# An attention block on one core: only the layer norm's result is turned, and the RMS factor moves to the values and to the floor of the norms

## The reference, cut to what matters

```
xn  = (x - mean) / sqrt(var + 1e-5)                      # layer norm, no weights
xh  = xn * rsqrt(mean(xn^2) + 2^-23) * norm_w            # RMS norm inside the attention
q, k, v = xh @ Wq, xh @ Wk, xh @ Wv                      # [256, 1024] each
q = q / max(|q|, 1e-12) * (q_gamma + 1) * 8              # per head
k = k / max(|k|, 1e-12) * (k_gamma + 1) * 8
p = softmax(tanh(q k^T / 50) * 50 / 8)
out = x + (p v) @ Wo + ffn(xn)
```

## Time and profile before

| | |
|---|---|
| instructions | 34237 |
| POOL busiest line | L1014, 256 times 1895 ns, 485.1 us |
| ACT busiest lines | L612 and L619, 256 times each, 265.4 and 272.8 us |
| longest waits, whole span | PEld L552 on issue 53.0 us, DVE L796 on PE 47.3 us, ACT L612 on PE 37.1 us |
| DMA | 85.44 MB moved, 310492 packets, 42.8% of the engines' time on the main queue |

### The profile page before, as it was taken

How to read it: one execution, slowest core, us unless ns; L and a number is a source line. 1 busy time by engine, 2 the same in 40 slices (tenths; PEclk the granted TensorE clock), 3 DMA queues, 4 the chain that set the end, 5 groups by cost and what they waited for, 6 DMA issues and landing times.

```text
span 1067.6 us, 34237 instructions
## 1 busy us (share of the span) xinstructions
PE 1033.9 (97%) x12889; PEld 844.5 (79%) x12889; DVE 938.0 (88%) x2217; ACT 976.3 (91%) x1417; POOL 981.2 (92%) x912
## 2 busy tenths in 40 slices
PE   6689999999999999999999999999999999999997
PEld 4468888888888888888888888888888888888877
DVE  5888999989999989999988999988999998999972
ACT  3689999999999999999999999999999999999996
POOL 6699999999999999999999999999999999999883
PEclk9899999999999999999999999999999999999999
DMA  3244434444453345544445444345444444444451
GB/s 117 46 86 73 90 81 73 76 87 82 85 81 80 72 84 86 82 82 76 83 76 87 84 80 81 72 86 90 79 82 82 77 78 90 77 86 73 72 99 31
DMA packets 310492, 85.44 MB, mean 80 GB/s; under 512 B 282021, under 2 KB 309817, under 8 KB 310329
## 3 DMA queue, kind: packets, MB, share of 16 engines
q1 hardware_dynamic: 310328, 83.25, 42.8%
HBM read 11.09 MB, written 4.19 MB: 14 GB/s over the span
## 4 chain that ended last, share of the span: by engine, by line
PE 43%; POOL 27%; issue 9%; SPq 6%; DVE 6%; ACT 4%; DMA 4%; POOLq 0%; ACTq 0%
POOL probs_lo L1014 11%; PE ps_scores L526 9%; PE ps_y L574 5%; PE ps_aux L501 4%; POOL sq_k L995 4%; POOL halves L1006 4%; PE ps_o L552 4%; PE ps_aux L512 4%; PE ps_aux L446 4%; DMA heads_T<-halves 3%; SPq L411 3%; PE ps_y L572 3%; PE ps_aux L448 3%; PE ps_aux L447 3%; SPq L399 2%
## 5 line engine op out<-in xcount | busy, mean ns | idle before, releaser
L1014 POOL TENSOR_TENSOR probs_lo<-probs 128x1024 f16<-128x1024 f32 x256 | 485.1, 1895 | 20.0 <-ACT probs L619 18.7
L612 ACT ACTIVATE clamped<-ps_scores 128x1024 f32<-128x1024 f32 x256 | 265.4, 1037 | 44.3 <-PE ps_scores L526 37.1
L619 ACT ACTIVATE probs<-clamped 128x1024 f32<-128x1024 f32 x256 | 272.8, 1066 | 3.0 <-PE ps_o L554 0.4
L552 PEld LDWEIGHTS ps_o<-v_hi,probs 128*128 128x128 bf16 x2048 | 183.9, 98 | 57.3 <-issue 53.0
L526 PE MATMUL ps_scores<-heads_T 64*128 64x256 f16 x3072 | 212.5, 271 | 5.3 <-ACT clamped L612 3.1
L552 PE MATMUL ps_o<-v_hi,probs 128*128 128x65 bf16 x2048 | 214.8, 195 | 2.8 <-POOL probs_lo L1014 1.6
L553 PE MATMUL ps_o<-v_lo,probs 128*128 128x64 bf16 x2048 | 212.4, 193 | 0.0
L554 PE MATMUL ps_o<-v_hi,probs_lo 128*128 128x65 bf16 x2048 | 211.8, 194 | 0.0
L446 PE MATMUL ps_aux<-w_hi,xhT_hi 128*128 128x512 f32 x384 | 176.1, 459 | 13.5 <-DVE qk L824 9.1
L553 PEld LDWEIGHTS ps_o<-v_lo,probs 128*128 128x128 bf16 x2048 | 187.8, 99 | 0.0
L554 PEld LDWEIGHTS ps_o<-v_hi,probs_lo 128*128 128x128 f16 x2048 | 187.7, 97 | 0.0
(11 more groups left out here) (85 smaller groups left out, 2001.8 us busy)
## 6 DMA issues: line engine op xcount, KB each, us to landing
heads_T<-halves SPq DMA_TRANSPOSE x512, 2.5
x_in<-in_L_attn_tokens_dram SPq DMA_DIRECT2D x32, 128.0 KB, 2.4
x_res<-in_L_attn_tokens_dram SPq DMA_DIRECT2D x32, 128.0 KB, 2.3
out_dram<-y_sb SPq DMA_DIRECT2D x32, 128.0 KB, 2.0
sel_raw<-xn SPq DMA_DIRECT2D x192, 4.0 KB
qk<-in_L_attn_Wkv_dram SPq DMA_DIRECT2D x2, 512.0 KB, 5.6
qk<-in_L_attn_Wq_dram SPq DMA_DIRECT2D x1, 512.0 KB, 3.6
qk<-in_L_ffn_W_dram SPq DMA_DIRECT2D x2, 256.0 KB
```

Source lines behind the costliest of these rows:

```text
L552: pe.matmul(full, hi[:, col], v_hi[:, par, u, h], start=(u == 0), stop=False)
L612: nc.scalar.activation(clamped[:].rearrange("p j n -> p (j n)"), ps_scores[:].rearrange("p j n -> p (j n)"), ACT.Tanh).then_inc(clamp_done, 1)
L619: nc.scalar.activation(probs[:, pair % RING].rearrange("p j n -> p (j n)"), clamped[:].rearrange("p j n -> p (j n)"), ACT.Exp, bias=LIFT, ...
L1014: g.tensor_tensor(probs_lo[:, buf].rearrange("p j n -> p (j n)"), probs[:, buf].rearrange("p j n -> p (j n)"), probs[:, buf].rearrange("p ...
```

## The change

xh is no longer made. Only xn is turned (two transposes instead of four), and ACT copies the same PSUM tile twice, into the fp32r tile for the projections and into the fp32 tile for the feed-forward block. The RMS factor, rstd[1], now is (1/(var+eps) * (var (1 + 2^-23) + 1e-5 2^-23))^-1/2, a number near one, and is multiplied in where v leaves PSUM: on ACT as the scale of an activation, on DVE as the scalar of a scalar_tensor_tensor. For q and k the floor of the squared norms is multiplied by the inverse of its square instead (`norm_floor`), one number for each token.

The two additions that POOL did before its power move to DVE's `norm_var`, in slot 4 behind the statistics and ahead of the read of q0, with a reciprocal and a product of two tiles; all four work on two elements for each partition, in SBUF. POOL keeps the power and adds one instruction for the floor. rstd and norm_floor are kept for four batches. The first instruction of `seed` becomes two, one for each token tile.

```
@@ norm tiles
-        rstd = sb("rstd", [P, 2, TT])
+        ms_eps = sb("ms_eps", [P, TT])
+        inv_eps = sb("inv_eps", [P, TT])
+        rstd = sb("rstd", [P, 4, 2, TT])
+        norm_floor = sb("norm_floor", [P, 4, TT])
-        xh = sb("xh", [P, TT, P])
@@ PE, aux "xT"
                     for t in range(TT):
-                        pe.transpose(bank[:, t * P:(t + 1) * P], xh[:, t], ident[:])
-                    for t in range(TT):
-                        ins = pe.transpose(bank[:, seq + t * P:seq + (t + 1) * P], xn[:, par, t], ident[:])
+                        ins = pe.transpose(bank[:, t * P:(t + 1) * P], xn[:, par, t], ident[:])
@@ ACT, aux
+                if kind == "v" and k == 0:
+                    act.wait_ge(rstd_made, b + 1)
-                    nc.scalar.copy(xnT[:, b % 3], bank[:, seq:2 * seq]).then_inc(xnT_copied, 1)
+                    nc.scalar.copy(xnT[:, b % 3], bank[:, 0:seq]).then_inc(xnT_copied, 1)
-                    nc.scalar.copy(v_hi[:, par, t, 8 * c:8 * c + 8, 0:DH],
-                                   bank.rearrange("p (h d) -> p h d", d=DH)).then_inc(v_hi_made, 1)
+                    nc.scalar.activation(v_hi[:, par, t, 8 * c:8 * c + 8, 0:DH],
+                                         bank.rearrange("p (h d) -> p h d", d=DH), ACT.Copy,
+                                         scale=rstd[:, b % 4, 1, t:t + 1]).then_inc(v_hi_made, 1)
@@ DVE, norm_var, behind its bn_aggr
+                dve.wait_ge(meanvar_made, 2 * b + 2)
+                wait(dve, floor_made, b)
+                v.tensor_scalar(var_eps[:, 0], mean_var[:, :, 1], LN_EPS, None, ALU.add).then_inc(vareps_made, 1)
+                v.tensor_scalar(ms_eps[:], mean_var[:, :, 1], 1.0 + RMS_EPS, RMS_EPS * LN_EPS,
+                                ALU.mult, ALU.add).then_inc(vareps_made, 1)
+                dve.wait_ge(vareps_made, 2 * b + 2)
+                v.reciprocal(inv_eps[:], var_eps[:, 0]).then_inc(inveps_made, 1)
+                dve.wait_ge(inveps_made, b + 1)
+                v.tensor_tensor(var_eps[:, 1], ms_eps[:], inv_eps[:], ALU.mult).then_inc(ratio_made, 1)
@@ DVE, seed
-                    v.tensor_scalar(minus_half_norm2, norm2[:], NORM2_MIN, -0.5, ALU.max, ALU.mult)\
-                        .then_inc(seed_made, 1)
+                    dve.wait_ge(floor_made, b + 1)
+                    half_of = TT * HEADS
+                    for t in range(TT):
+                        part = slice(t * half_of, (t + 1) * half_of)
+                        v.tensor_scalar(minus_half_norm2[:, part], norm2[:, part], norm_floor[:, b % 4, t:t + 1], -0.5,
+                                        ALU.max, ALU.mult).then_inc(seed_made, 1)
@@ DVE, aux "v"
-                    v.tensor_tensor(v_lo[:, par, t, 8 * c:8 * c + 8], bank.rearrange("p (h d) -> p h d", d=DH),
-                                    v_hi[:, par, t, 8 * c:8 * c + 8, 0:DH], ALU.subtract).then_inc(v_split, 1)
+                    v.scalar_tensor_tensor(v_lo[:, par, t, 8 * c:8 * c + 8], bank.rearrange("p (h d) -> p h d", d=DH),
+                                           rstd[:, b % 4, 1, t:t + 1], v_hi[:, par, t, 8 * c:8 * c + 8, 0:DH],
+                                           ALU.mult, ALU.subtract).then_inc(v_split, 1)
@@ POOL, norm_rstd
-                pool.wait_ge(meanvar_made, 2 * b + 2)
-                wait(pool, rstd_made, b)
-                g.tensor_scalar(var_eps[:, 0], ...).then_inc(vareps_made, 1)
-                g.tensor_scalar(var_eps[:, 1], ...).then_inc(vareps_made, 1)
-                pool.wait_ge(vareps_made, 2 * b + 2)
+                pool.wait_ge(ratio_made, b + 1)
                 wait(pool, xn_made, b)
+                wait(pool, v_split, 4 * (b - 3))
                 g.tensor_tensor(rstd[:, b % 4]..., var_eps..., minus_half[:], ALU.pow).then_inc(rstd_made, 1)
+                wait(pool, seed_made, 3 * (b - 3))
+                g.tensor_scalar(norm_floor[:, b % 4], var_eps[:, 1], NORM2_MIN, None, ALU.mult).then_inc(floor_made, 1)
@@ POOL, norm_apply
-                g.tensor_tensor(xn[:, par], x_mid[:], rstd[:, 0]..., ALU.mult)
-                g.tensor_tensor(xh[:], x_mid[:], rstd[:, 1]..., ALU.mult).then_inc(xn_made, 1)
+                g.tensor_tensor(xn[:, par], x_mid[:], rstd[:, b % 4, 0]..., ALU.mult).then_inc(xn_made, 1)
```

More of the change, by code:

```diff
@@ L274, in block_kernel @@
         seed_made = sem("seed_made")
+        ratio_made = sem("ratio_made")
+        inveps_made = sem("inveps_made")
+        floor_made = sem("floor_made")
         newton_step = sem("newton_step")
@@ L738, in seed @@
                     wait(dve, newton_step, 9 * b)
-                    v.tensor_scalar(minus_half_norm2, norm2[:], NORM2_MIN, -0.5, ALU.max, ALU.mult)\
-                        .then_inc(seed_made, 1)
+                    dve.wait_ge(floor_made, b + 1)
[4 more added lines that the diff above has]
+                                        ALU.max, ALU.mult).then_inc(seed_made, 1)
                 else:
-                    dve.wait_ge(seed_made, 2 * b + 1)
+                    dve.wait_ge(seed_made, 3 * b + 2)
                     v.tensor_scalar(newton_r[:].bitcast(I32), minus_half_norm2.bitcast(I32), -0.5, RSQRT_SEED,
@@ L749, in newton @@
                 if k == 0:
-                    dve.wait_ge(seed_made, 2 * b + 2)
+                    dve.wait_ge(seed_made, 3 * b + 3)
                 wait(dve, newton_step, 9 * b + k)
@@ L826, in aux @@
                 elif kind == "v":
+                    if k == 0:
+                        dve.wait_ge(rstd_made, b + 1)
                     dve.wait_ge(v_hi_made, 4 * b + k + 1)
                     t, c = k // 2, k % 2
-                    v.tensor_tensor(v_lo[:, par, t, 8 * c:8 * c + 8], bank.rearrange("p (h d) -> p h d", d=DH),
-                                    v_hi[:, par, t, 8 * c:8 * c + 8, 0:DH], ALU.subtract).then_inc(v_split, 1)
+                    v.scalar_tensor_tensor(v_lo[:, par, t, 8 * c:8 * c + 8], bank.rearrange("p (h d) -> p h d", d=DH),
+                                           rstd[:, b % 4, 1, t:t + 1], v_hi[:, par, t, 8 * c:8 * c + 8, 0:DH],
+                                           ALU.mult, ALU.subtract).then_inc(v_split, 1)
                 elif kind == "low":
@@ L922, in norm_rstd @@
                 b, _, _ = st.batch(ahead)
-                pool.wait_ge(meanvar_made, 2 * b + 2)
-                wait(pool, rstd_made, b)
-                g.tensor_scalar(var_eps[:, 0], mean_var[:, :, 1], LN_EPS, None, ALU.add).then_inc(vareps_made, 1)
-                g.tensor_scalar(var_eps[:, 1], mean_var[:, :, 1], 1.0 + RMS_EPS, RMS_EPS * LN_EPS,
-                                ALU.mult, ALU.add).then_inc(vareps_made, 1)
-                pool.wait_ge(vareps_made, 2 * b + 2)
+                pool.wait_ge(ratio_made, b + 1)
                 wait(pool, xn_made, b)
-                g.tensor_tensor(rstd[:].rearrange("p a b -> p (a b)"), var_eps[:].rearrange("p a b -> p (a b)"),
+                wait(pool, v_split, 4 * (b - 3))
+                g.tensor_tensor(rstd[:, b % 4].rearrange("p a b -> p (a b)"), var_eps[:].rearrange("p a b -> p (a b)"),
                                 minus_half[:], ALU.pow).then_inc(rstd_made, 1)
+                wait(pool, seed_made, 3 * (b - 3))
+                g.tensor_scalar(norm_floor[:, b % 4], var_eps[:, 1], NORM2_MIN, None, ALU.mult).then_inc(floor_made, 1)
             def norm_apply(st, ahead):
@@ L940, in norm_apply @@
                 pool.wait_ge(mid_made, b + 1)
-                g.tensor_tensor(xn[:, par], x_mid[:], rstd[:, 0].unsqueeze(2).to_broadcast([P, TT, P]), ALU.mult)
-                g.tensor_tensor(xh[:], x_mid[:], rstd[:, 1].unsqueeze(2).to_broadcast([P, TT, P]), ALU.mult)\
+                g.tensor_tensor(xn[:, par], x_mid[:], rstd[:, b % 4, 0].unsqueeze(2).to_broadcast([P, TT, P]), ALU.mult)\
                     .then_inc(xn_made, 1)
```

## The result

The changed kernel is slower: 1148.59 us median (1142.17 to 1154.88, 6 runs) against 1064.97 us (1063.91 to 1068.36, 6 runs) for the kernel before in the same runs. The ratio is 1.0788, 95% interval 1.0762 to 1.0813. The prediction was 1123 us with a range of 1053 to 1132: the direction and the mechanism held, the size was 58 us where 84 were lost, and the time lies outside the range. The profiled execution took 1142.94 us, with a span of 1141.0.

What follows compares the result with a forecast made beforehand. PE was taken to bound the kernel. Per batch 2.38 - 0.22 - 0.15 = +2.01 us, 29 times, less 0.66, gave +57.6 us; on 1069.78 us, less 4.1, that made 1123 us, range 1053 to 1132.

Steps and rivals of the forecast that it cites:

- What bounds the kernel: PE paces each 31.76 us batch and loses 0.33 us at k3; DVE is 0.3 us behind it at one place.
- The four instructions on DVE: norm_var, held by POOL's instructions ahead of q0's read, makes v1 on PE late: +2.38 us a batch, bounds 0 to 2.38.
- first rival: At norm_var the product gets in just ahead of POOL's L1014: +0.31 us a batch, 1074 us; chance 0.18.
- second and third rivals: At norm_var, only the product is held, by L1006 (1064 us, chance 0.10), or nothing is held (1057 us, chance 0.24).
- the multiplication by 29: 29 of 32 batches counted at +2.01 us each, less 0.66 for the first three batches' transposes: +57.6 us.
- The last step of the sum: Profiled execution's 1069.78 us plus 57.6 gives 1127.4; taking off its 4.1 us above the median gives 1123.
- The gains, -0.22 and -0.15: Per batch: two fewer PE transposes, -0.22 us; POOL's earlier squares of k shorten k3's wait, -0.15 (0 to -0.33).
- ACT's copies, counted 0 with at most 0.06 us: ACT's four copies of v become scaled activations, 595 to 609 ns each: counted 0, at most 0.06 us a batch.
- The free room at q0's read, 0.77 us: DVE's read of q0 could start 0.77 us late before v1 on PE is delayed.
- third rival: Two-column operations at norm_var are not held; q0's read 0.60 us late, -0.27 us a batch, 1057 us; chance 0.24.

Runs made afterwards that it cites:

- Experiments 1 to 4: Changed kernel with sums and product one column at a time: 1062.84 us; only the product: 1103.22; only the sums: 1081.26; kernel before plus the four instructions, results unread: 1140.76.
- Experiment 6, after_one_row: Changed kernel with only one of the six small row transfers of each batch: 1132.98 us, ratio to before 1.0637.
- experiment 4: Kernel before plus the same four DVE instructions, written into tiles that nobody reads: 1140.76 us, ratio 1.0707.
- experiment 12: As both_early, with the two transposes of each batch put back: 1055.52 us, ratio to before 0.9910.
- both_early: As k0_early, with DVE's read of q2 moved ahead of the low parts: 1056.68 us, ratio to before 0.9922.
- Experiment 8: Changed kernel with sums and product one column at a time, behind q0's read, and v left unscaled: 1054.93 us, against 1061.65 with the scaling.
- k0_early: Changed kernel with sums and product one column at a time, behind q0's read, and ACT's copy of k0 ahead of the exp: 1057.62 us.
- narrow_all: Changed kernel with the two sums and the product one column at a time, at the same place: 1062.84 us, ratio to before 0.9975.

## Why the prediction was wrong

**What bounds the kernel.** Right as far as it went: PE set the period of the kernel before and lost 0.33 us at k3. That DVE was only just behind it was seen, but then used for one place alone.

**The four instructions on DVE.** Right, and nearly to the size. Forecast: first sum held to the end of the second L1006, product ready as L1014 starts and held to its end, q0's read 3.0 us late, v1 2.28 us late plus 0.10. Measured in the ordinary batch: 3.10 us (443.10 against 440.00, which is 0.06 behind L720), 2.35 plus 0.10. The product came 0.13 us behind the start of POOL's instruction, so the first rival lost by about the error of the working: that part was a near thing, not something that the working could decide. Experiments 1 to 4 show that the hold is the cause, that both forms are subject to it, and that even two columns are; that settles the second and third rivals too. The rule of the Trainium skill's "SBUF — State Buffer", section "Who interferes with whom", by which the second to issue waits for the first, agrees with the 0.95 and 1.79 us of the ordinary batch; the 3.5 us holds go beyond it, since there two POOL instructions that start after the sum has been issued pass ahead of it. The case of two elements in the Trainium skill's "Vector Engine (DVE) Microarchitecture Reference", section "5.1 Performance modes — why throughput varies by op and dtype", agrees with the sum's 0.95 us.

**The step that failed: the multiplication by 29.** "29 * 2.01 - 0.66 = +57.6 us" takes the batch of 491 to 523 us for every batch. For the ordinary batch the term measured 2.04, 59 us for 29. The profiled execution lost another 16 us in the long batches, for which the sum has no term. Two things stand there. The first is the length of the hold: when a late head has pushed POOL's instructions together, the first sum is held for 3.5 us in place of 0.95, or the second for 1.94 in place of 0.15 (about 11 of the 19.9 us, an estimate). The second is the TensorE clock, which the prediction does not name and so puts at nothing: in 5 of the 29 batches the granted clock fell to 0.50 around PE's wait at v1 (about 9 us, from the same estimate). Experiment 6 separates them: without the late heads no long hold is left, the long batches cost 10.4 us in place of 19.9, and each of the seven that are left has its stretch at the lower clock.

The trace of before had signs of both. The second L843 of the earlier trace rows was not let in between L942 and L976, although three POOL instructions ended in that time, and in five steps POOL waits 1.04 to 1.66 us for a transposed head in slot 2; these are its five long batches. I used the first only for the moment of release and left the second out. Between 28 and 60 us, where PE waits for DVE for up to 3.2 us, the mean granted clock was 0.84. One batch stood for all, and my range had no room for a tail.

The last step of the sum failed too. The profiled execution of before was 4.1 us above its median, and I took these 4.1 us off; the profiled execution of the changed kernel is 5.6 us below its own. That is 9.7 of the 25.6 us between 1123 and 1148.59. The other five runs of the changed kernel had a mean granted clock of 0.975 to 0.978, the profiled one 0.990, but one of the five was as fast as the profiled one (1142.17 us), so the clock alone does not order them.

**The gains, -0.22 and -0.15.** Both too good. The transposes do not count in the changed kernel (experiment 4, 33.86 to 33.80), since PE waits at v1, and do not count in the quick form either (experiment 12). There DVE's waits for the values' PSUM tile come to 30.1 us in the whole trace of both_early, against 47.3 before: DVE has less room left, and I take it, without a run that shows it, that DVE sets the pace in part.

**ACT's copies, counted 0 with at most 0.06 us.** Wrong: 0.095 us each, 0.38 in a batch, and two of them stand in the chain to k0's copy and v3. Experiment 8 prices the scaled evictions, ACT's and DVE's together, at 6.7 us; that it is ACT's place in the chain rests on k0_early, which keeps them and gains 0.25 us a batch. The activation with a fixed scale (L638, 609 ns) was the nearest row by form, but it has no per-partition operand; what such an operand adds was visible on DVE (742 for 687).

**The free room at q0's read, 0.77 us.** Near right. In narrow_all the read comes 0.94 us later than before and v1 starts 0.21 late, so 0.73 us were free; beyond that comes the 0.10 for the weight load. But the four instructions and their three more take 0.94 us there, not the 0.60 that the third rival gave four, and so the unheld form pays 0.31 us at v1.

What stays open: why the changed kernel has more steps with a late head than the kernel before with the same four instructions (7.8 us between their medians), and why the granted clock falls in some batches and not in others with the same 2.2 us wait at v1.

## What to carry to other kernels

Before you move a small operation to VectorE in a kernel whose GpSimd is busy, look at where its tiles lie and how many columns it has: two SBUF inputs, or a two-column tensor_scalar from SBUF to SBUF, cost what is left of the GpSimd instruction beside it (0.4 to 3.5 us here for 0.15 us of work), while one column at a time costs nothing of the kind. When a wait depends on another engine's gaps, look at those gaps over the whole trace before you multiply one batch's wait by the number of batches. A wait of PE can cost more than its length: behind some of the 2.2 us waits here the granted clock fell to the lower level, for another 1.5 us each time, so read the granted clock of the long batches before you look for another wait. And where four engines are within some per cent of each other, a cut on the one that looks like the bound (0.22 us of PE in a batch) may be worth nothing, and a tenth more on one that does not (ACT's 0.095 us) may be worth it in full.

## What the runs showed of the hardware

- A two-column tensor_scalar from SBUF to SBUF on DVE lasts until the GpSimd instruction beside it ends (0.95 us at the median, up to 3.51 us through three instructions that follow each other without a gap). A one-column one was never held (narrow_all: 64 of 64 of the first sums between 142 and 155 ns), nor a two-column reciprocal (0.17 us in all of them).
- A tensor_tensor of two columns with both inputs in SBUF ends with the GpSimd instruction, 1.78 to 1.80 us in the ordinary batches, and takes 0.16 us when GpSimd is idle.
- A per-partition scale raises an ACT copy of 128x512 from PSUM from 595 to 690 ns, and a DVE operation of 128x512 takes 745 ns in the three-operand form with a per-partition scalar, 687 ns in the two-operand form.
- The first operation of `seed` on 32 columns takes 245 ns with its per-partition floor, more than the 218 ns of the 64-column one without.
- The granted TensorE clock fell from 1.00 to 0.50 around a PE wait of 2.1 to 3.2 us for DVE in 5 of the 29 batches of the changed kernel and in 8 of after_one_row; in the other batches it stayed at 1.00 behind waits of the same length. At 0.50 a pass of 512 columns comes every 0.42 us, at 1.00 every 0.24, and such a stretch costs about 1.5 us here.
